# Two transformer layers written out instead of looped, their feed-forward cut into chunks, and two small steps of a tile moved between engines

## The reference

```python
def _layer(x, wqkv, qs, ksc, wo, lg, lb, w1, b1, w2, b2):
    h = shift_token(x)                      # channels 64.. come from the token before
    q, k, v = split(h @ wqkv, 3)            # 8 heads of 64
    q = l2norm(q) * qs; k = l2norm(k) * ksc
    q, k = rotary_xpos(q, k)                # q*cos*scale + rotate_half(q)*sin*scale, likewise k
    o = local_attention(q, k, v)            # windows of 64 keys: the own one and the one before
    x = x + o @ wo
    h = layernorm(shift_token(x)) * lg + lb
    a, g = split(h @ w1 + b1, 2)            # 341 + 341 columns
    return x + (a * gelu(g)) @ w2 + b2
```

## Time and profile before

| | us |
|---|---|
| time, median of 3 runs (lowest to highest) | 1568.89 (1566.64 to 1571.5) |
| the profiled execution: its own time / its span | 1564.41 / 1562.6 |
| stretch D in the span (first shift to the end) | 1078 to 1562.6 |
| layer 0 / layer 1 / output norm and store | 234.3 / 234.2 / 16 |
| mean granted TensorE clock over the span | 0.943 |

### The profile page before, as it was taken

How to read it: one execution, slowest core, us unless ns; L and a number is a source line. 1 busy time by engine, 2 the same in 40 slices (tenths; PEclk the granted TensorE clock), 3 DMA queues, 4 the chain that set the end, 5 groups by cost and what they waited for, 6 DMA issues and landing times.

```text
span 1562.6 us, 24586 instructions
## 1 busy us (share of the span) xinstructions
PE 1352.1 (87%) x9009; PEld 799.1 (51%) x9009; DVE 1042.3 (67%) x2249; ACT 782.3 (50%) x1668; POOL 386.9 (25%) x264
## 2 busy tenths in 40 slices
PE   6999999999999999995899999872788867788866
PEld 4767676776777653332233333331466642466642
DVE  5766867687676848755766766408788645788644
ACT  4544544444444423341366666752677732677731
POOL 0000000010000014354200000002788800788801
PEclk9999999999999999996699999996899978899978
DMA  5000000000000000011122111002000000000000
GB/s 136 1 1 1 1 1 1 0 1 1 0 1 0 1 0 1 1 51 55 62 63 72 36 36 35 3 10 52 1 0 0 1 1 1 1 0 0 1 1 27
DMA packets 23672, 25.75 MB, mean 16 GB/s; under 512 B 5570, under 2 KB 20108, under 8 KB 22284
## 3 DMA queue, kind: packets, MB, share of 16 engines
q1 hardware_dynamic: 23580, 24.51, 5.4%
HBM read 20.11 MB, written 4.39 MB: 16 GB/s over the span
## 4 chain that ended last, share of the span: by engine, by line
PE 58%; POOL 16%; DVE 11%; issue 8%; ACT 5%; DMA 1%; POOLq 0%; SPq 0%; DVEq 0%; ACTq 0%
PE ps L698 12%; PE ps L718 8%; PE ps L733 6%; POOL d_rn L2383 5%; PE ps L1070 4%; POOL probsT L2394 4%; PE ps L1029 4%; PE ps L1050 3%; POOL q_st L2381 2%; DVE negmax L1401 2%; POOL k_st L2381 2%; PE ps L907 2%; PE ps L901 2%; PE ps L669 2%; PE ps L1273 2%
## 5 line engine op out<-in xcount | busy, mean ns | idle before, releaser
L2122 ACT ACTIVATE probsT<-ps 128x512 f32<-128x512 f32 (+1 forms) x304 | 163.6, 575 | 103.4 <-PE ps L1054 91.5
L1401 DVE TENSOR_REDUCE negmax<-ps 128x1 f32<-128x1024 f32 x128 | 150.7, 1219 | 72.3 <-PE ps L718 72.1
L1944 ACT ACTIVATE probs<-ps,negmax 128x1024 f32<-128x1024 f32 x128 | 142.7, 1115 | 80.5 <-DVE negmax L1401 76.6
L1950 ACT COPY probsT<-ps 128x512 f32<-128x512 f32 x128 | 74.9, 585 | 168.1 <-PE ps L733 168.0
L733 PEld LDWEIGHTS ps<-ident,probs 128*128 128x128 f32 x1024 | 114.7, 141 | 66.0 <-issue 43.8
L733 PE MATMUL ps<-ident,probs 128*128 128x128 f32 x1024 | 138.6, 277 | 6.6 <-DVE probsT L1414 3.3
L1029 PE MATMUL ps<-arena 76*128 76x512 bf16 (+3 forms) x384 | 113.7, 355 | 26.2 <-DVE cmax L1669 20.6
L2254 POOL TENSOR_SCALAR rstd<-mv 128x8 f32<-128x8 f32 (+1 forms) x11 | 2.6, 238 | 535.7 <-DVE mv L1336 535.6
L718 PE MATMUL ps<-k_st,q_st 64*128 64x512 f32 x512 | 128.5, 620 | 5.9 <-ACT probs L1944 5.9
L1669 DVE CUSTOM_DVE_ANT_0 k_st<-ps,rel 128x256 f32<-128x256 f32 (+7 forms) x128 | 96.8, 756 | 43.9 <-PE ps L1029 43.0
L1669 DVE CUSTOM_DVE_ANT_0 q_st<-ps,rel 128x256 f32<-128x256 f32 (+7 forms) x128 | 96.7, 756 | 41.7 <-PE ps L1029 40.7
(11 more groups left out here) (255 smaller groups left out, 2636.0 us busy)
## 6 DMA issues: line engine op xcount, KB each, us to landing
arena<-c_parts SPq DMA_DIRECT2D x32, 192.0 KB
arena<-c_parts SPq DMA_DIRECT2D x16, 128.0 KB
arena<-in_L_ffn_w_dram SPq DMA_DIRECT2D x3, 512.0 KB
c_parts<-probsT SPq DMA_DIRECT2D x2, 768.0 KB, 3.5
arena<-in_c_far_dram SPq DMA_DIRECT2D x16, 96.0 KB
c_parts<-work SPq DMA_DIRECT2D x2, 768.0 KB, 11.2
work<-in_L_ffn_wqkv_dram SPq DMA_DIRECT2D x1, 1536.0 KB
x_sb<-in_L_attn_x_dram SPq DMA_DIRECT2D x2, 512.0 KB, 5.8
```

The costliest lines, as they stand in the source:

```text
L1401: dve.tensor_reduce(negmax[:, u:u + 1], s2, AX_X, ALU.max, negate=True).then_inc(s_a_negmax, 1)
L1944: act.activation(probs[:, u % NPB, :], s2, ACT.Exp, bias=negmax[:, u:u + 1], accum_out=rowsum[:, u:u + 1]).then_inc(s_a_exp, 1)
L2122: act.activation(c_p[:, kt % 2, j0:j0 + heads, q0 - kt * P:q0 - kt * P + n], ps[:, 4 + c % 2, 0:heads * n].rearrange("p (h n) -> p h n", n ...
```

## The change

**No loops.** Both layers and all tiles of stretch D are written out. The per-layer copies of weights, biases and shifted input (`l_qkv`, `l_up`, `l_down`, `l_o`, `l_b`, `hq`, `hv`) are gone; instructions read the stacked weights and `hT` where they lie. The product buffer `gbuf` has a place of its own in the arena.

**In a tile.** The addition of rotated products is halved: POOL adds the queries' 512 columns, DVE the keys' (`add_keys`). The copy of the old values into `d_vs` moves from DVE to ACT, ahead of the copies of the new values. DVE no longer copies tiles of `hT`.

**Feed-forward and norms by chunks of 512 tokens.** `shift` works on a chunk. The norms ahead of the feed-forward are done chunk by chunk; `1/sqrt` comes from POOL (`half_rstd`, the helper that the first blocks use: an addition and a power). Chunks 0 and 1 are shifted in steps 12 and 13, normalised in step 14, and their first three pairs of up matmuls stand in steps 15 to 17. The gate and up banks go round a ring. Projections, squares, rotations and tables of the next layer's first tiles stand between the matmuls of the last chunks. The second layer has the output norm of each chunk there instead, and four DMAs of 256 KB store the result. The next layer's second rotation table is made just ahead of its first step. `proj_qk` now waits for its chunk of `hT` (`s_d_hT`) and reads `hT` and `w4qkv` in place.

```diff
+SPREADS += [("ffn", l, b, g) for l in range(DEPTH) for b in range(BATCH) for g in range(HALF)]
+SPREADS += [("out", 3, b, g) for b in range(BATCH) for g in range(HALF)]
...
-                             x_sb[:, b * QT:(b + 1) * QT, :]).then_inc(s_out, 16)
-            sp.wait_ge(s_out, 16 * BATCH)
+                for g in range(HALF):
+                    sp.wait_ge(s_res, group_no(3, b, g))
+                    sp.dma_start(out[b, g * CH:(g + 1) * CH].rearrange("(t p) d -> p t d", p=P),
+                                 x_sb[:, tiles_of(b, g), :]).then_inc(s_out, 16)
+            sp.wait_ge(s_out, 16 * NCH)
...
+        def ring(j):
+
+            return (0, 1) if j == 0 else (6, 7) if j == 1 else (4, 5) if j % 2 == 0 else (2, 3)
...
+            def up(l, j):
+
+                c, m = j // 3, j % 3
+                r, n = M1[m]
+                gate_bank, up_bank = ring(j)
+                x = yT[:, c * CH:(c + 1) * CH]
+                pe.wait_ge(s_f_yT, NCH * l + (c + 1 if j else 2))
+                if j == 1:
+                    pe.wait_ge(s_d_e, TILES * (l + 1))
+                if j == 3:
+                    pe.wait_ge(s_d_z, TILES * (l + 1) + 1)
+                if j >= 4:
+                    pe.wait_ge(s_f_u, 3 * NCH * l + j - 1)
+                pe.matmul(ps[0:n, gate_bank, :], w4up[:, l, HID + r:HID + r + n], x, start=True, stop=True)\
+                  .then_inc(s_f_g, 1)
+                pe.matmul(ps[0:n, up_bank, :], w4up[:, l, r:r + n], x, start=True, stop=True).then_inc(s_f_a, 1)
...
+            def last_out(c):
+
+                pe.wait_ge(s_f_z, NCH + c + 1)
+                if c >= 2:
+                    pe.wait_ge(s_yn, group_no(3, c // 2 - 1, c % 2))
+                half_out(3, c // 2, c % 2, c % 2, xT)
...
+                pe.wait_ge(s_d_sq, TILES * (l + 1))
+                ffn_in(l, 0, 0)
+                ffn_in(l, 1, 1)
+                step(l, 14)
+                ffn_turn(l, 0, 0)
+                step(l, 15, lambda: ffn_turn(l, 1, 1))
+                up(l, 0)
+                up(l, 1)
+                step(l, 16)
+                up(l, 2)
+                step(l, 17)
+                pe.wait_ge(s_f_u, 3 * NCH * l + 1)
+                ffn_in(l, 2, 0)
+                up(l, 3)
+                ffn_in(l, 3, 1)
+                up(l, 4)
+                ffn_turn(l, 2, 0)
+                up(l, 5)
+                down(l, 0)
+                up(l, 6)
+                ffn_turn(l, 3, 1)
+                up(l, 7)
+                up(l, 8)
+                down(l, 1)
+                pe.wait_ge(s_f_yT, NCH * (l + 1))
+                if last:
+                    last_out(0)
+                else:
+                    proj_qk(l + 1, 0)
+                up(l, 9)
+                up(l, 10)
+                up(l, 11)
+                down(l, 2)
+                if last:
+                    last_out(1)
+                else:
+                    proj_qk(l + 1, 1)
+                down(l, 3)
+                if last:
+                    last_out(2)
+                    last_out(3)
+                else:
+                    proj_qk(l + 1, 2)
 
...
+            def add_keys(l, t):
+                    n, par = TILES * l + t, t % 2
+                    dve.wait_ge(s_d_m, n + 1)
+                    dve.tensor_tensor(d_kq[par][:, INNER:2 * INNER], d_mA[:, par, INNER:2 * INNER],
+                                      d_mB[:, par, INNER:2 * INNER], ALU.add).then_inc(s_d_addk, 1)
...
-
-                        if exists(t, -1):
-                            dve.wait_ge(s_d_v, n)
-                            if exists(t, -2):
-                                dve.wait_ge(s_d_o, n - 1)
-                            dve.tensor_scalar(d_vs[WIN:P, par, :], d_va[WIN:P, 1 - par, :], 0.0, None, ALU.add)\
-                               .then_inc(s_d_vs, 1)
-                        else:
-                            dve.sem_inc(s_d_vs, 1)
...
+                        add_keys(l, t + 2)
+                        norms(l, t + 2)
...
-                    if exists(t, 4):
-                        copy_hq(t + 4, par)
-                    if exists(t, 1):
-                        copy_hv(t + 1, 1 - par)
+                    if piece:
+                        piece()
                     if exists(t, 0):
                         dve.wait_ge(s_d_e, n + 1)
                         dve.reciprocal(d_rr[:, par, :], d_sum[:, par, :]).then_inc(s_d_rr, 1)
...
+            add_keys(0, 1)
+            norms(0, 1)
+            for l in range(DEPTH):
+                last = l == DEPTH - 1
+                for t in range(12):
+                    step(l, t)
+                step(l, 12, lambda: shift(0, s_f_hT))
+                step(l, 13, lambda: shift(1, s_f_hT))
+
+                def first_stats():
+
+                    ffn_stats(l, 0)
+                    ffn_stats(l, 1)
+                    ffn_xn(l, 0)
+                    ffn_xn(l, 1)
+
+                step(l, 14, first_stats)
+                step(l, 15, lambda: shift(2, s_f_hT))
+                step(l, 16)
+                gated(l, 0)
+                gated(l, 1)
+                step(l, 17)
+                dve.wait_ge(s_d_z, TILES * (l + 1) + 1)
+                shift(3, s_f_hT)
+                gated(l, 2)
+                ffn_stats(l, 2)
+                gated(l, 3)
+                ffn_xn(l, 2)
+                ffn_stats(l, 3)
+                gated(l, 4)
+                gated(l, 5)
+                add_down(l, 0)
+                ffn_xn(l, 3)
+                gated(l, 6)
+                if not last:
+                    tables(l + 1, 0)
+                gated(l, 7)
+                if not last:
+                    next_shift(l, 0)
+                gated(l, 8)
+                add_down(l, 1)
+                if last:
+                    last_stats(0)
+                else:
+                    ch.settle()
+                    rotate(l + 1, 0)
+                gated(l, 9)
+                if last:
+                    last_norm(0)
+                else:
+                    add_keys(l + 1, 0)
+                    norms(l + 1, 0)
+                gated(l, 10)
+                if not last:
+                    next_shift(l, 1)
+                gated(l, 11)
+                add_down(l, 2)
+                if last:
+                    last_stats(1)
+                    last_norm(1)
+                    add_down(l, 3)
+                    last_stats(2)
+                    last_norm(2)
+                    last_stats(3)
+                    last_norm(3)
+                else:
+                    rotate(l + 1, 1)
+                    add_down(l, 3)
+                    add_keys(l + 1, 1)
+                    norms(l + 1, 1)
+                    next_shift(l, 2)
+                    next_shift(l, 3)
+                    tables(l + 1, 1)
+                    ch.settle()
...
+                    if piece:
+                        piece()
                     if exists(t, 0):
+                        if exists(t, -1):
+                            act.wait_ge(s_d_v, n)
+                            act.copy(d_vs[WIN:P, par, :], d_va[WIN:P, 1 - par, :])
                         act.wait_ge(s_d_vp, n + 1)
-                        if exists(t, -1):
-                            act.wait_ge(s_d_vs, n)
                         act.copy(d_va[:, par, :], ps[:, 3, :])
                         act.copy(d_vs[0:WIN, par, :], ps[0:WIN, 3, :]).then_inc(s_d_v, 1)
...
+                step(l, 15, both_yT)
+                step(l, 16, lambda: gelu(l, 0))
+                gelu(l, 1)
+                step(l, 17)
+                for j in range(2, 3 * NCH):
+                    gelu(l, j)
+                    if j == 4:
+                        ffn_yT(l, 2)
+                    if j == 6:
+                        ffn_yT(l, 3)
+                    if l + 1 < DEPTH:
+                        if j == 8:
+                            square(l + 1, 0)
+                if l + 1 < DEPTH:
+                    square(l + 1, 1)
+                    act.activation(tpre[:, 1:2], eps_c[:, 0:1], ACT.Exp)
+                    square(l + 1, 2)
...
-                    pool.tensor_tensor(kq, d_mA[:, par, :], d_mB[:, par, :], ALU.add).then_inc(s_d_add, 1)
+                    pool.tensor_tensor(kq[:, 0:INNER], d_mA[:, par, 0:INNER], d_mB[:, par, 0:INNER], ALU.add)\
+                        .then_inc(s_d_add, 1)
                     pool.wait_ge(s_d_cl, n + 1)
                     pool.tensor_tensor(d_rn[:, par, :], ss[:, par, :], half_c[:, :], ALU.pow).then_inc(s_d_rn, 1)
-                    pool.wait_ge(s_d_add, n + 1)
+                    pool.wait_ge(s_d_addk, n + 1)
                     pool.wait_ge(s_d_rn, n + 1)
                     v = kq[:, INNER:2 * INNER].rearrange("p (h d) -> p h d", d=HD2)
                     pool.tensor_tensor(v, v, d_rn[:, par, H2:2 * H2].unsqueeze(2).to_broadcast([P, H2, HD2]), ALU.mult)\
                         .then_inc(s_d_kq, 1)
 
...
+            for l in range(DEPTH):
```

(13 more changed lines are left out.)

381 lines of the change are left out of this document (151 added, 230 removed).

## The result

| | before | after |
|---|---|---|
| time, median of 4 runs each (lowest to highest) | 1567.77 (1566.38 to 1571.5) | 1509.86 (1507.81 to 1511.4) |
| the profiled execution: its own time / its span | 1564.41 / 1562.6 | 1508.53 / 1506.5 |
| mean granted clock over the span | 0.943 | 0.957 |

The ratio is 0.9626 (95% interval 0.9603 to 0.9649): 57.9 us less by the medians, 56.1 by the two spans. The forecast was 1516, with 53 us less.

What follows compares the result with a forecast made beforehand. The prediction took POOL and a bubble as the bound, with a floor of 8.92 us a tile. Gains of 1.9 + 12.6 + 26 + 12.5 = 53 us gave 1511.4 for the profiled execution, 1516 as median; range 1502 to 1540.

Steps and rivals of the forecast that it cites:

- the bubble: In the loop's tiles: 1.06 us a tile lost, because DVE's copy of old values delays the rotation in even tiles.
- the floor: In a tile: 8.92 us, set by a ring of ACT, PE and DVE, not by POOL's sum.
- ACT's copy "at nothing": In a tile: ACT's added copy of some 0.5 us costs nothing, covered by 1.5 us idle; otherwise 13 us.
- The eleven periods: In the tiles of a layer: eleven periods fall from 9.49 to 8.92 us, 6.3 us gained a layer.
- Start: At tile 0 of layer 0: without copies of weights, the rotation's wait and small DVE copies go, 1.9 us gained.
- Between the layers: Tile 13's reciprocal to layer 1's first: a step-by-step walk gave 82.3 against 110.4 us; 26 us gained was taken.
- End: After tile 13 of layer 1: walk gave 79.8 against 93.7 us; 12.5 of the 13.9 us gain was taken.
- The port: Rival, in a tile: DVE's new addition waits for POOL's SBUF access, +28.6 us, 1545; chance 0.10.
- The loop's period: Rival, in the tiles: the period stays at 9.49 us, so 12.6 us is missing, 1529; chance 0.08.
- Code: Rival, written-out stretch D: 41 more instruction packets stall engines, 1577 at 1.5 us each, slower than before; chance 0.03.
- The clock: Rival, both feed-forwards: PE runs a third of them at half rate, 20.6 us more, 1537; chance 0.07.
- the list of signs: Expected profile: reciprocals 8.9 us apart, POOL idle over 1.3, key addition 0.68, 84 us between layers, 80 at the end.

Runs made afterwards that it cites:

- e2: The changed kernel, but DVE copies the old values ahead of the rotation and ACT doesn't: median 1507.0 us, ratio to before 0.9615, tile 8.92 us.
- e11: The changed kernel, but ACT copies only 64 of the 512 columns of the old values: median 1511.8 us, ratio to before 0.9638, tile 9.04 us.
- e12: The changed kernel, but DVE adds the keys' half right behind the reciprocal, beside POOL's multiplication: median 1510.8 us, ratio to before 0.9632.
- e9: The changed kernel, but the feed-forward's first two chunks stand behind step 17 in both layers: median 1532.6 us, ratio to before 0.9762.

## Why the prediction was right

**Bound and floor.** "POOL is in the chain, the bubble belongs to the late copy, the floor is 8.92." The bubble was DVE's copy, as said, but its reason was not found: it was held 1.4 to 1.7 us by POOL's multiplication. I had read one row of such a collision and sought it in the added operation, not in the one taken away. The period came to 9.04. The floor of 8.92 is real (e2), and the missing 0.12 is ACT's copy. But the floor was put down to a ring of ACT, PE and DVE, and in e2 it is PE's own work in a tile.

**ACT's copy "at nothing".** This term was mis-sized: 0.12 us a tile, 3.1 in all. The cover that I named held for its duration (ACT is still idle 0.73 behind it) and did not help (e11). The eleven periods gave 4.4 us a layer and not 6.3. That the gain was still 6.0 and 6.4 is luck. One more bubble stood behind tile 1, where the sum had none (9.94 before, 9.04 after, 0.9 a layer), and the period behind R0 was shorter by 0.75 and 1.16 (11.07 and 10.20 before, 10.32 and 9.04 after). That last part goes with the granted clock, which was 0.69 and 0.83 there before and 0.83 and 1.00 after.

**Start.** 1.9 was forecast, 0.0 came. The rotation of tile 0 did start 0.9 us earlier (1086.64 against the earlier trace rows), not 1.9: the shift, now four chunks of two copies, took 3.55 us of DVE's queue (1077.87 to 1081.42) instead of 2.69 (1078.06 to 1080.75), where I had counted 3. Then the rest was lost on PE. It had been idle 6.53 us ahead of the second projection instead of 3.62, and both later ones ran at a granted clock of 0.50 (1089 to 1093 and 1096 to 1100) where the kernel before had 0.57 (1090 to 1094 and 1097 to 1101), 3.75 us each instead of 3.35 and 3.49:

```profile
1078.88 3.75 PE L1130 MATMUL ps<-work,arena 128*128 128x512 f32 x4 [5.39 <-DVE arena L1754]
1089.16 3.75 PE L1130 MATMUL ps<-work,arena 128*128 128x512 f32 x4 [6.53 <-DVE probs L1782]
1096.53 3.75 PE L1130 MATMUL ps<-work,arena 128*128 128x512 f32 x4 [3.61 <-DVE probs L1782]
```

**Between the layers.** The walk gave 28.1, I took 26 for hand-offs, 28.3 came. Its marks: last tile added at 32 by the walk, at 30.8 in the trace; PE's last projection done at 69 against 68.2 (1294.79 + 1.96 - 1228.54); next R0 at 82.3 against 82.0. The two inserted steps cost 11.8 and 10.6 us a tile, and the head was DVE's queue, as the walk has it. The allowance for hand-offs was not needed here; in the sum it made the forecast 2.1 us too small.

**End.** Walk 13.9, taken 12.5, came 15.3. The last addition ended 75.6 us behind R13 (1502.48 + 1.26 - 1428.12) where the walk had 76, and the span 2.8 behind it where I had 3.8. That is 1.4 us, and my allowance was another 1.4.

**The sum and the base.** 56.1 came for 53. The other 3 of the 6 us by which the median is below 1516 are the base: I added 4.5 us for the distance of the profiled execution to the median, and after's is 1.3.

**Rivals.** The port: the added operation goes free under the power and would go free ahead of POOL (e12); the collision was in the old copy. The loop's period: the tile went to 9.04, so it fell, though the loop did have a part in the bubble. Code: 12 and 9 more packets, not 41, and the steady tiles repeat within 0.01 us. The clock: 1.00 in both feed-forwards (layer 1: 1.00 from 1460 to 1497, 0.89 in its foot); within this change the lower level came into the up matmuls only when the chunks were moved back (e9), but tile 15 took 1.2 us more in layer 1, at 0.79, than in layer 0, at 1.00. POOL's idle time, the key addition, the matmuls and the 84 us were as the list of signs said, the period wasn't.

## What to carry to other kernels

Where an operation of DVE inside SBUF takes two or more durations in a trace, lay it beside POOL's rows: if it starts just behind one of POOL's and ends with it, the order of the two starts, here 0.05 us one way or 0.06 to 0.39 the other, decides over 1.4 to 1.7 us. A step moved to an idle engine may cost more than its time shows. When work is inserted into a ring, put it behind the operation that the other engines wait for: that alone gave 6.3 us here. And where the same code takes different times in two places, read the granted clock there first.
